# A loop over four passes written out pass by pass, in a two-layer language-model tower on one Trainium2 core

## The reference

```python
h = _L0_tok_ref(x, W_E)                          # rows of the embedding table, times 16
h = h + _L0_attn_ref(_layernorm(h), ...)         # RWKV time mix and channel mix
h = h + _L0_ffn_ref(_layernorm(h), ...)          # 8 experts of 256->1024->256, top 2 of 8
h = h + _L1_attn_ref(_layernorm(h), ...)         # RWKV recurrence with a running maximum
h = h + _L1_ffn_ref(_layernorm(h), ...)          # 16-head causal attention, then 4 experts, top 2
```

## Time and profile before

| | us |
|---|---|
| median of 3 runs | 3230.91 (3225.17 to 3234.37) |
| the profiled execution | 3222.42 |
| its span, first to last instruction | 3220.4 |
| PE busy | 2778.5 (86% of the span) |
| ACT busy | 1785.4 (55%) |
| DVE busy | 1695.8 (53%) |
| POOL busy | 1407.7 (44%) |

### The profile page before, as it was taken

How to read it: one execution, slowest core, us unless ns; L and a number is a source line. 1 busy time by engine, 2 the same in 40 slices (tenths; PEclk the granted TensorE clock), 3 DMA queues, 4 the chain that set the end, 5 groups by cost and what they waited for, 6 DMA issues and landing times. The chain is left out here.

```text
span 3220.4 us, 58240 instructions
## 1 busy us (share of the span) xinstructions
PE 2778.5 (86%) x21884; PEld 1859.2 (58%) x22208; DVE 1695.8 (53%) x3163; ACT 1785.4 (55%) x2819; POOL 1407.7 (44%) x1326
## 2 busy tenths in 40 slices
PE   3787866898899999999999999999999998987778
PEld 1454544565665566566655665566656665663555
DVE  6777754636444635463446344635464446446552
ACT  2444534555665566656655665566556655664634
POOL 5454522443445444544454444444544343453334
PEclk8898987999999999999999999999999999999999
DMA  2000004842112122222222222222222222110002
GB/s 67 14 13 26 13 14 165 322 171 71 66 67 78 69 71 76 91 73 72 72 91 70 72 76 80 81 71 76 79 83 71 70 73 73 53 53 27 24 22 74
DMA packets 59721, 235.94 MB, mean 73 GB/s; under 512 B 6560, under 2 KB 25024, under 8 KB 40640
## 3 DMA queue, kind: packets, MB, share of 16 engines
q1 hardware_dynamic: 57920, 228.13, 20.3%
q0 software_dynamic: 1536, 4.20, 0.5%
HBM read 200.57 MB, written 31.72 MB: 72 GB/s over the span
## 5 line engine op out<-in xcount | busy, mean ns | idle before, releaser
L1381 POOL TENSOR_TENSOR c_lo<-c_g,c_hi 128x512 bf16<-128x512 f32 x720 | 888.2, 1241 | 1341.8 <-ACT c_hi L1543 1216.9
L2220 PE MATMUL c_up<-c_xT,c_ring 128*128 128x512 bf16 x2855 | 707.4, 384 | 78.4 <-ACT c_hi L1543 52.4
L2237 PE MATMUL c_down<-c_ring,c_hi 128*128 128x256 bf16 x4096 | 714.7, 275 | 0.0
L1542 ACT ACTIVATE c_g<-c_up,b 128x512 f32<-128x512 f32 x512 | 353.2, 690 | 491.5 <-PE c_up L2220 487.7
L2237 PE MATMUL c_down<-c_ring,c_lo 128*128 128x256 bf16 x2048 | 563.2, 275 | 0.0
L2220 PEld LDWEIGHTS c_up<-c_xT,c_ring 128*128 128x128 bf16 x3072 | 294.7, 99 | 362.3 <-ACT c_hi L1543 64.1
L2237 PEld LDWEIGHTS c_down<-c_ring,c_hi 128*128 128x128 bf16 x4096 | 397.4, 98 | 106.2 <-issue 1.7
L1543 ACT ACTIVATE c_hi<-c_up,b 128x512 bf16<-128x512 f32 x512 | 351.1, 686 | 0.0
L1809 DVE CAST c_room<-c_room 128x384 bf16<-128x384 f32 x256 | 127.1, 528 | 403.2 <-PE c_front L2132 307.8
L1542 ACT ACTIVATE c_g<-c_up 128x512 f32<-128x512 f32 x176 | 105.5, 600 | 291.7 <-PE c_up L1973 285.6
L2237 PEld LDWEIGHTS c_down<-c_ring,c_lo 128*128 128x128 bf16 x2048 | 201.5, 98 | 25.4
(11 more groups left out here) (334 smaller groups left out, 5439.2 us busy)
## 6 DMA issues: line engine op xcount, KB each, us to landing
c_ring<-kept_dense SPq DMA_DIRECT2D x112, 1024.0 KB, 4.8
c_ring<-kept_experts SPq DMA_DIRECT2D x63, 512.0 KB, 3.3
c_room<-in_WB SPq DMA_DIRECT2D x16, 1024.0 KB, 7.1
kept_dense<-c_ring SPq DMA_DIRECT2D x16, 1024.0 KB, 4.8
c_ring<-kept_experts SPq DMA_DIRECT2D x28, 384.0 KB, 3.4
kept_experts<-c_room SPq DMA_DIRECT2D x9, 512.0 KB, 4.1
c_xT<-kept_xT SPq DMA_DIRECT2D x8, 512.0 KB, 4.7
out<-h SPq DMA_DIRECT2D x8, 512.0 KB, 6.5
```

Of the source, the lines that this page charges most:

```text
L1381: pool.tensor_tensor(lo14[:, a, :], g[:, h % 4, :], hi14[:, a, :], ALU.subtract).then_inc(lo_ready.sem, 1)
L1542: act.activation(g[:, h % 4, :], ub[n % 2][:, :], ACT.Gelu, bias=bias)
L2220: last = pe.matmul(ub[n % 2][:, :], r[:, wp, o + q * P:o + (q + 1) * P], xT[:, xp, q, :], start=(m == 0 and q == 0), stop=(m == 2 and q == ...
L2237: m = pe.matmul(bank, (hi14, lo14)[xp][:, a, s * P:(s + 1) * P], r[:, wp, o + KC * P:o + CHUNK], start=False, stop=(k == HC0 - 1 and n == ...
```

## The change

Both `Fori` loops become Python loops. The body is emitted four times on each of the five instruction streams, with `i` = 3, 4, 5 and 6 as constants. Nothing else is changed; where the code asks `isinstance(i, int)`, the values 3 to 6 give what the register's branch gives.

```diff
@@ -1177,7 +1177,7 @@
             go(ORDER_0, splits, dense(0, PLAN_B, None))
             go(ORDER_B, dense(1, PLAN_B, PLAN_B), front(0))
             go(ORDER_BC, dense(2, PLAN_BC, PLAN_B), front(1), gates(0))
-            with eng.Fori(3, TILES - 1) as i:
+            for i in range(3, TILES - 1):
                 go(ORDER_BC, dense(i, PLAN_BC, PLAN_BC), front(i - 1), gates(i - 2))
@@ -1301,7 +1301,7 @@
             streamed(2, PLAN_BC, PLAN_B)
-            with sp.Fori(3, TILES - 1) as i:
+            for i in range(3, TILES - 1):
                 streamed(i, PLAN_BC, PLAN_BC)
```

## The result

| | before | after |
|---|---|---|
| median of 4 runs, us | 3232.64 (3225.17 to 3235.13) | 3202.68 (3202.06 to 3207.99) |
| the profiled execution | 3222.42 | 3202.13 |
| its span | 3220.4 | 3200.2 |

The ratio is 0.9908, with an interval of 0.9896 to 0.9920: faster, by 0.92%.

What follows compares the result with a forecast made beforehand. PE's stream was taken to set each pass's length. Passes 3 to 6 were to fall from 1293.93 to 1279.2 us, a gain of 14.7, 8.25 of it jumps: 3230.91 - 14.7 = 3216.2, range 3205 to 3227.

Steps and rivals of the forecast that it cites:

- the sum's last line: Whole kernel: gain of 14.7 us taken off the runs' median of 3230.91, which lay 8.5 above the profile, giving 3216.2.
- 4 x 318.31 gives 20.7: Passes 3 to 6: upper bound of the gain, 20.7 us, if no written-out pass has a low-clock stretch.
- They lie in the shadow of PE and count for nothing by themselves: Jumps of ACT, DVE and POOL fall away too, but were given no gain of their own.
- The jump, 8.25: Start of passes 4 to 6: PE's jump back costs 2.66, 2.77 and 2.82 us; removing it gains 8.25.
- The register work, 2.12 a pass: Loop passes: register instructions on the path cost 2.12 us a pass, from comparing pass 2 with pass 3.
- I can't tell it for the new passes: Written-out passes: which idle time of PE is followed by a low clock could not be foretold.
- The four lengths given (318.31 to 321.29): Written-out passes 3 to 6: possible lengths 318.31, 319.30, 320.30 or 321.29 us, depending on low-clock stretches.
- The choice of 319.8: Written-out pass length used in the sum: 319.8 us, the middle of 319.30 and 320.30, the two clock patterns seen.
- Instruction blocks: PE's fetch queue: about 20 blocks a pass after the change, against 22 in pass 4 in the loop.
- (a): Rival: the gap at PE's jump is not the jump and stays; only 6.5 us gained, time 3224.4; chance 6%.
- (b): Rival: low clock in every pass takes the register gain; gain 8.8 us, time 3222.1; chance 12%.
- (c): Rival: slower, written-out code fetched late at block boundaries in PE's stream, up to 2.8 us each; time 3238.6; chance 5%.

Runs made afterwards that it cites:

- profile 1: The kernel before, unchanged, the profiled execution the prediction rests on: 3222.42 us, passes 3 to 6 together 1293.93.
- profiles 2 to 4 of before: Three further profiles of the unchanged kernel before: passes 3 to 6 take 1301.7, 1305.2 and 1304.8 us.
- e1: Against the kernel before, passes 3 to 6 each in a loop of one trip, on all engines: 3204.5 us.
- e12: The changed kernel with phase_a's loops written out too, third group: 3199.00 us, 23.0 below the kernel before on that chip.
- e16: The changed kernel with phase_a's loops written out too, fourth group: 3202.71 us, against 3206.05 for the changed kernel on that chip.
- fourth group: Runs on one chip of the kernel before (twice), the changed kernel, and that with phase_a written out; median of before 3234.01 us.
- third group: Runs on another chip, on ACT's wait order, DVE's loop edge and phase_a written out; median of before 3222.02 us.
- e7: The changed kernel, but DVE alone keeps the loop: median 12.1 us above the kernel where only POOL loops; passes 3 to 6 cost 14.2 more than changed.
- e2: Against the kernel before, only PE's stream written out with constants, the other engines keep the loop: 3235.91 us, ratio 1.0016.
- e3: Against the kernel before, ACT, DVE, POOL and SyncE written out, PE alone keeps the loop: 18.7 us below before.
- e6: The changed kernel, but ACT alone keeps the loop: median 16.6 us above the kernel where only POOL loops; passes 3 to 6 cost 16.1 more than changed.
- e9: The changed kernel with ACT's two waits ahead of an activation swapped, in all passes: ratio 1.0010 to the kernel before.
- e15: The changed kernel, unchanged, run beside the kernel before on the fourth group's chip: 3206.05 us against 3234.01.
- e5: Against the kernel before, passes 3 to 6 as two loops of two trips, so pass 5 begins without a jump: 3230.23 us.
- e11: The changed kernel, but DVE alone loops, its loop beginning mid-pass at token A0, with two jumps instead of three: 3208.99 us.
- e10: The kernel before, loops kept, with ACT's two waits ahead of an activation swapped: 3223.73 us against 3222.02 for before.
- e13: The kernel before, unchanged, its third profile, on the fourth group's chip: passes 3 to 6 take 1305.2 us; median of before there 3234.01.

## Why the prediction was wrong, step by step

**The failed step: the sum's last line.** The prediction says "The median of the runs is 8.5 us above it (3230.91); the forecast for the median is 3230.91 - 14.7". That takes the distance between profile and median for something that the change leaves alone. It was part of what the change removes. The gain measured from profile 1 to the changed kernel is 15.8, and the profiles 2 to 4 of before have a mean of 1303.9 for passes 3 to 6, against 1278.3 (mean of the changed kernel's two): 25.6 us of the 30.0. The remaining 4.4 stay unexplained. The 10 us between profile 1 and the others go with stretches of low clock in the passes that the change touches: 27 us in profile 1, 48 to 58 in the others, 27 to 31 in every one of the changed kernel's five profiles (with e1, e12 and e16). Those 4 to 6 us behind the mark follow the jump's gap, which the change removes. Those between 173 and 200 us follow an idle time that the change leaves as it is (1.95 us); that none of them follows it any more is counted, not explained. In these passes the five profiles lie within 1.4 us of each other, the four of before within 11.3. Without the clock the change gives less: profile 1 and e12 both have 27.3 us of low clock and differ by 1293.9 - 1277.0 = 16.9 us. How much comes on top depends on the chip or the execution: the median of before lies 31.3 us above e16's in the fourth group, and 23.0 above that of the same kernel, e12, in the third. A sign of it was on the table: the profile's 3222.42 lay below the lowest of the three runs, 3225.17.

**The bound "4 x 318.31 gives 20.7"** fell with it. Its upper end came from how short a written-out pass can be, and that was right: the shortest seen is 318.05. It left out how long the loop's passes could be.

**"They lie in the shadow of PE and count for nothing by themselves"** was wrong on mechanism. ACT's and DVE's loops cost 16.1 and 14.2 us alone, PE's 5.5; without the clock, by the pass lengths above, about 8, 10 and 9. That the forecast from profile 1 still met 15.8 is because pass 2 against pass 3 measured all engines at once: the lump was right, its parts were not. Nor do the parts add up: 16.1 + 14.2 + 5.5 + 0.1 = 35.9, more than the sum of any profile of before over 1278.2 (15.7 to 27.0). DVE's jump and PE's happen at the same time, and each covers the other: at the start of pass 4 of before PE is idle for 2.63 us by its own jump and 2.46 more for ACT, 5.09 together, where e7, with DVE's jump alone, has 5.59. That fits e2, where PE's jumps are gone and nothing is gained.

**The jump, 8.25.** The gap, its cause and its absence after are confirmed. At equal clock patterns: 324.2 (before, passes 4 to 6) less 319.27 (changed, pass 6) less 2.15 for the register work gives 2.8 a jump, the 2.66 to 2.82 forecast. PE's jump alone gives the same (e3, 3.0). But it isn't PE's gap alone: DVE's own costs about as much where PE's isn't there (e7).

**The register work, 2.12 a pass.** Confirmed as a size: pass 3 of before and pass 6 of the changed kernel have the same clock pattern (low at 54 and 218 us behind the mark) and differ by 321.42 - 319.27 = 2.15. As a cause it was misread. PE's instructions cost nothing (e3, pass 3). It is ACT's, 2.0 of it (e6, pass 3), and by where a wait stands and not by its length: e9 has no register in these passes and loses as much and more, most of it by the clock.

**The clock: "I can't tell it for the new passes".** The four lengths given (318.31 to 321.29) hold for all 20 written-out passes 3 to 6 of the changed kernel, e15, e1, e12 and e16 (318.05 to 320.49), but for 0.3 us at the lower end. The choice of 319.8 was near: their mean is 319.4.

**The rest.** Instruction blocks: 20 on the fetch queue in pass 4, as forecast, and the count over the launch fell from 176 to 169.

```profile
q8 instruction: 20, 0.33, 0.4%
```

**The rivals.** (a) fell with the gap. (b) fell: the clock didn't take the gain, it added to it. (c) fell: PE has no idle time ended by "issue" at the start of passes 3 to 6 any more, and the written-out passes agree to 2.4 us. None of them said "more than the forecast", and that was the side the time came out on.

**What stays open.** Why one execution of the kernel before has its low clock behind an idle time and another hasn't, and why the same idle time in the changed kernel never has. The runs show only where: at places whose idle time is followed by 1.2 GHz in some executions, and which places those are depends on the loop (the counts above). Whether profile 1 came from a chip like that of the third group, or was one fast execution among slower ones, isn't known either. What PE's jump costs with the other engines' jumps in place was not isolated; e5 was meant to.

## What to carry to other kernels

When one profile lies outside the spread of the timed runs, don't carry the distance over as a constant: take a second profile, or allow in the range for a gain that scales with it. An engine that is idle half the time still sets the pace if its loop jumps, or its table load waits, at the one spot where the busiest engine hangs on it. Ask of each engine what it does right after the loop's edge. Before writing a loop out, look at the order of the waits ahead of a table load, and at the token where a loop begins: in e11 moving DVE's edge takes its cost in the profile from 14.2 us to 3.4, though the runs confirm only a part of that, and in e10 turning the waits around alone gained no time. When two executions are compared, compare their clock patterns first: here a few us of low clock more or less hide an effect or double it.

## What the runs showed of the hardware

- DVE is idle 4.42 to 4.60 us behind a taken jump of this long body (e7), though its branch record is short (63 ns), like ACT's; PE's record holds the time itself (3.4 to 3.8 us in the four profiles of before). The same branch in the short body of `phase_a` has a record of 76 to 247 ns on PE. "Advanced Engine Details and Errata", Control Flow Timing, in the Trainium skill, gives about 108 ns for a compare-and-branch; neither DVE's idle time nor PE's record is near that when the branch is taken back over a pass.
- A table load (1283 ns) waits with whatever wait is placed ahead of it, and of two waits before an activation a constant and a register count put a different one there (for the register, inferred from when the load starts). Turning the two waits around in two places costs 20 us here (e9), the low clock that came with it included.
- The same idle time of PE (1.95 us, 180 us behind the mark) is followed by the lower clock in some executions and not in others (e13 and profile 1 of before), and in none of the 40 passes counted above in which ACT's load doesn't wait.
- A loop of one trip leaves no register arithmetic in the trace (94 of PE's 942 records, e1).
